# Second feed-forward on tiles of 128 rows, its norm computed during the attention

## Chip, cores and metric

One NeuronCore of a Trainium2 chip runs one program. The metric is the device time of one execution in microseconds (us); lower is better. Several runs of a kernel give a median.

## What is computed

x has 32 batches of 112 rows of 256 numbers, the context 32 batches of 375 rows of 256. Four layers follow one another, each added to x: an attention with one head over the context, a feed-forward of six linear maps, an attention with 16 heads over the context, and a second feed-forward. The last two are what the change touches:

```python
x = x + _L1_xattn_ref(ctx_1024, _layernorm(x), w_q, w_kv, w_out, b_out)      # 16 heads of 16
x = x + _L1_ffn_ref(_layernorm(x), norm1_w, w1, act_scale, act_bias, norm2_w, w2)

def bitlinear(x, norm_w, w):
    x_norm = rmsnorm(x, norm_w)                     # x / sqrt(mean(x*x) + 1e-8) * norm_w
    x_q = activation_quant(x_norm)                  # per row: round(x * 127 / max|x|), clipped, scaled back
    w_q = weight_quant(w)                           # -1, 0 or 1, times mean|w|
    return einsum('bsd,hd->bsh', x_q, w_q)
h = bitlinear(x, norm1_w, w1)                       # 256 -> 1024
h = act_scale * square(relu(h)) + act_bias
y = bitlinear(h, norm2_w, w2)                       # 1024 -> 256
```

## The kernel before

The program writes out the instructions of five engines by hand: TensorE (`pe`), ScalarE (`act`), VectorE (`dve`), GpSimd (`pool`) and SyncE (`sp`), which issues every DMA. Each engine executes its own list in order; a semaphore wait holds all that stands behind it on that engine. Four stages are separated by `stage_end` (L283), at which each engine waits for all others: setup, first attention, first feed-forward with the queries, second attention; the second feed-forward comes last.

x lies in SBUF for the whole program as `xs` (tile name x_stream), 112 partitions by 32 batches by 256. So every step works on one batch, 112 of 128 partitions.

**Second attention.** One step per batch b (`over_thirds`, three sets of buffers, loops of three batches). TensorE (`step3`, L1699) weaves the scores of batch b with `scores_for_max` of the batches b+1 and b+2, the weighing of the values, and the end of batch b-1: `fin_rows`, `fin_turn`, `fin_project`. VectorE takes the maxima of the score rows (`maxima`, L1188), splits them in three bf16 parts (`parts_m`), normalises the heads (`norm_o`), adds the output to x (`x4`, L1211, which raises `x_after_attn2`) and takes its statistics (`stats4`, `aggregate4`, `keep4`). GpSimd lays out the values (`lay_v`, L645) and computes from the statistics the factors of the later norm (`factors4`, L653, six linked operations on one column). `scores` of a batch needs `minus_max_in_place`: the row maxima, copied by ScalarE (`m_out`) and moved into `qs` by one small DMA (`rows_m`, L495).

SyncE runs `moves` (L512) for each batch:

```python
            def moves(b, par, n):
                more = not isinstance(b, int) or b < B - 3
                if more:
                    sp.wait_ge(shifted_scores_made, 12 * b + 6)
                    load_half(b + 3, par, 0)      # six DMAs
                if not isinstance(b, int) or b < B - 1:
                    rows_m(b + 1, (par + 1) % 3)
                if more:
                    sp.wait_ge(shifted_scores_made, 12 * b + 12)
                    load_half(b + 3, par, 1)      # six DMAs
```

**Second feed-forward.** After the barrier SyncE loads the two norm vectors. Per batch: GpSimd applies the norm to the row (`rms_x`, L713, three operations of 256 columns) and computes the root of the hidden norm (`hidden`, L726). VectorE finds the row maximum, rounds and clips (`max_x`, `factor_x`, `factors_x`, `round_x`, `clip_x`). TensorE turns the rows (`in_turn`), ScalarE copies them (`xq_out`), TensorE multiplies (`in_product`). ScalarE: `relu`, `square`, `squares` (sum of squares). VectorE: `activate` (L1277), `weigh_h` (L1306), `max_h` (L1310), `factors_h`, ScalarE `shift_up`, VectorE `clip_h`, TensorE `out_turn`, ScalarE `hq_out` (L919), TensorE `out_product` (L1757), VectorE `result` (L1337), SyncE `store_out`. In its step TensorE (L1765) runs `in_turn(b+1)`, `in_product(b+1)`, `out_product(b-2)`, `out_turn(b-1)`. VectorE's step (L1343) runs the twelve kinds above for the batches b+2, b, b-1 and b-2.

Of the kernel before, what the change touches and what calls it, by code (L numbers as in the profile page):

```python
# [11 lines left out]
P = 128  # L12
# [5 lines left out]
def xattn_ffn_kernel(  # L18
# [8 lines left out]
    TC = 3  # L27
# [17 lines left out]
    LN_EPS, RMS_EPS, Q_EPS = 1e-5, 1e-8, 1e-5  # L45
    assert TP * TC == T and KS + 3 <= P and NG % 2 == 0 and B % 2 == 0

    kd = nc.dram_tensor("k_parts_dram", [B, 3, DH, H, T], BF16, kind="Internal").ap()
    qd = nc.dram_tensor("q_parts_dram", [3, B, KC, DH, H8, L], BF16, kind="Internal").ap()

    with ExitStack() as ctx:
# [16 lines left out]
        w1T = sb("w1T", [P, KC, HID], BF16)  # L68
        w2T = sb("w2T", [P, HC, D], BF16)
# [6 lines left out]
        rs4, t4, rr4 = (sb(n, [L, B]) for n in ("rs4", "t4", "rr4"))  # L76
        eps4 = sb("eps4", [P, 2])
# [15 lines left out]
        wffT = eb("wffT", [P, NLIN, KC, D])  # L93
        b1parts = eb("b1parts", [P, NBLK, D], BF16)
# [51 lines left out]

        s3 = ExitStack()
# [8 lines left out]
        pvs = b3("pvs", [P, HQ, L])  # L156
        on = b3("on", [L, D])
        rden = b3("rden", [L, H])
        oT = pvs[:, 0:KC, :]
        nm = b3("nm", [L, H])  # L160
        nres = b3("nres", [L, H])
        npart = b3("npart", [L, 6 * H], BF16)
        mrow = b3("mrow", [6 * H, L], BF16)
        bs3 = b3("bs3", [L, 6])
        mv3 = b3("mv3", [L, 2])
# [3 lines left out]
        def b4(name, shape, dt=F32):  # L169
            return alloc(s4, name, shape, dt)  # L170
        n1_bc = b4("n1_bc", [P, D])
        n2_bc = b4("n2_bc", [P, HID])
        sc4 = b4("sc4", [L, B])
        nms4 = b4("nms4", [L, B])
        fw = b4("fw", [P, 2])
        y4 = [b4(f"y4{i}", [L, D]) for i in range(2)]
        xr4 = b4("xr4", [L, D])
        yw4 = b4("yw4", [L, D])
        am4 = [b4(f"am4{i}", [L, 13]) for i in range(2)]
        xq4 = b4("xq4", [L, D])  # L180
        xqT = b4("xqT", [P, KC, L], BF16)
        th = [b4(f"th{i}", [L, HID]) for i in range(2)]
        uh = [b4(f"uh{i}", [L, HID]) for i in range(2)]
        gh = [b4(f"gh{i}", [L, HID]) for i in range(2)]
        sq4 = b4("sq4", [L, HID])
        hq4 = b4("hq4", [L, HID])
        roundc = b4("roundc", [P, 1])
        hqT = b4("hqT", [P, HC, L], BF16)
        ot4 = [b4(f"ot4{i}", [L, D]) for i in range(2)]
        s4.close()  # L190


        at = [0]
# [1611 lines left out]
```

## Time and profile before

| | |
|---|---|
| median of 3 runs | 1369.27 us (1363.68 to 1371.06) |
| the profiled execution | 1369.87 us |
| its span | 1368.1 us |
| busy: TensorE, VectorE, ScalarE, GpSimd | 1172.6, 960.0, 596.2, 443.6 us |
| second attention | about 738 to 1130 us |
| second feed-forward | about 1134 to 1368 us |

The page of the profile gives the busy share of each engine in forty slices of the span, the granted TensorE clock (PEclk, 1.00 is 2.4 GHz, 0.50 is 1.2 GHz) and what the DMA engines moved. The timeline lists instructions by their start, with a bracket for the idle time before them and what ended it; SPq marks the instructions with which SyncE issues a DMA. Groups by form collect all instructions of one line and shape, with the mean duration. L numbers are lines of the kernel; L1405 is a helper that several products share.

### The profile page before, as it was taken

How to read it: one execution, taken by the hardware profiler on the slowest of the kernel's cores; microseconds unless marked ns; L12 is line 12 of the kernel's file. 1: busy time of each engine (PE TensorE's matmuls, PEld its weight loads, DVE VectorE, ACT ScalarE, POOL GpSimd, SP SyncE). 2: the span in 40 equal slices, each digit the busy share in tenths (PEclk: the TensorE clock that was granted, in tenths of full speed). 3: DMA queues.
4: the chain of work that ended last, by engine and by line, in shares of the span. 5: the costliest groups of instructions: out<-in, count | busy, mean ns of one | idle time of the engine just before them, and what ended most of it. 6: DMA issues, size and time to landing. Idle time of an engine off the chain costs nothing. (4 is left out here: it accounts for less than half of the span.)

```text
span 1368.1 us, 30729 instructions
## 1 busy us (share of the span) xinstructions
PE 1172.6 (86%) x9322; PEld 799.6 (58%) x9322; DVE 960.0 (70%) x2495; ACT 596.2 (44%) x1009; POOL 443.6 (32%) x792
## 2 busy tenths in 40 slices
PE   2799999999996989889666999999999993666766
PEld 2677777887775566565432555555555551444544
DVE  3556656666654666675556788888888864999996
ACT  1322232322231111111242556565565663888886
POOL 0334444444432221221113122222222224454451
PEclk7599999999998999999896999999999995777786
DMA  9323333223320000000069556566565610000000
GB/s 222 93 57 89 94 96 88 84 84 91 95 83 17 1 0 0 0 0 1 14 146 168 118 121 126 116 127 129 117 125 116 130 25 19 14 20 17 17 17 24
DMA packets 105310, 99.26 MB, mean 73 GB/s; under 512 B 43923, under 2 KB 98742, under 8 KB 105270
## 3 DMA queue, kind: packets, MB, share of 16 engines
q1 hardware_dynamic: 105270, 98.76, 31.3%
q8 instruction: 20, 0.33, 0.1%
q14 instruction: 20, 0.16, 0.0%
HBM read 70.76 MB, written 27.61 MB: 72 GB/s over the span
## 5 line engine op out<-in xcount | busy, mean ns | idle before, releaser
L1190 DVE TENSOR_REDUCE nm<-bank 112x1 f32<-112x375 f32 x512 | 269.9, 545 | 41.5 <-PE bank L1645 37.3
L864 ACT ACTIVATE pT<-bank 125x448 f32<-125x448 f32 x384 | 202.1, 543 | 96.6 <-PE bank L1661 93.8
L1645 PE MATMUL bank<-ks,qs 96*128 96x375 bf16 x512 | 171.5, 338 | 18.7 <-POOL qs L681 17.1
L1675 PE MATMUL bank<-pT,vaug 125*32 125x112 f32 x3072 | 152.7, 272 | 0.0
L1661 PE MATMUL bank<-qs,ks 128*128 128x112 bf16 x1536 | 141.8, 215 | 3.3 <-DMA qs<-mrow 3.0
L1661 PEld LDWEIGHTS bank<-qs,ks 128*128 128x128 bf16 x1536 | 97.6, 99 | 47.5 <-issue 31.2
L1675 PEld LDWEIGHTS bank<-pT,vaug 125*32 125x32 f32 x3072 | 60.7, 108 | 72.3 <-issue 59.7
L815 ACT ACTIVATE yT<-bank,bcol,gcol 128x448 f32<-128x448 f32 x48 | 32.2, 721 | 160.3 <-PE bank L1545 160.3
L1563 PE MATMUL bank<-wffT,hT 128*112 128x256 f32 x384 | 99.3, 392 | 0.0
L1405 PE MATMUL bank<-wv1T,ctxT 128*125 128x256 f32 x384 | 88.0, 379 | 0.0
L1405 PE MATMUL bank<-ctxT,wk1T 128*128 128x375 f32 x256 | 86.0, 478 | 0.0
L1089 DVE BATCH_NORM_STATS2 bs<-bank 112x6 f32<-112x256 f32 x96 | 36.6, 423 | 64.7 <-PE bank L1563 64.7
L1405 PEld LDWEIGHTS bank<-wv1T,ctxT 128*125 128x125 f32 x384 | 71.9, 187 | 17.3
L666 POOL TENSOR_TENSOR t<-mv,eps 112x1 f32 (+1 forms) x32 | 6.1, 191 | 230.1 <-DVE mv L1229 230.1
L1645 PEld LDWEIGHTS bank<-ks,qs 96*128 96x128 bf16 x512 | 50.2, 99 | 51.5 <-issue 39.6
L796 ACT ACTIVATE pr<-bank,ebias 112x375 f32<-112x375 f32 x32 | 18.4, 573 | 141.1 <-DVE ebias L1041 141.1
L1405 PE MATMUL bank<-yT,wffT 128*128 128x448 f32 x192 | 76.2, 540 | 0.1
L1545 PE MATMUL bank<-ident,yn 112*128 112x112 f32 x320 | 41.8, 278 | 37.9 <-DVE yn L1098 20.7
L1563 PEld LDWEIGHTS bank<-wffT,hT 128*112 128x112 f32 x384 | 64.0, 184 | 15.8 <-issue 1.8
L1405 PE MATMUL bank<-w1T,xqT 128*112 128x512 bf16 x128 | 48.9, 522 | 26.4 <-ACT xqT L917 26.4
L1545 PEld LDWEIGHTS bank<-ident,yn 112*128 112x128 f32 x320 | 34.1, 149 | 57.9 <-DVE yn L1098 35.9
L1405 PEld LDWEIGHTS bank<-ctxT,wk1T 128*128 128x128 f32 x256 | 48.4, 189 | 32.8
(210 smaller groups left out, 2451.3 us busy)
## 6 DMA issues: line engine op xcount, KB each, us to landing
k_parts_dram<-kp SPq DMA_DIRECT2D x192, 93.8 KB, 3.5
ks<-k_parts_dram SPq DMA_DIRECT2D x64, 281.2 KB, 4.2
cnat<-in_ctx_dram SPq DMA_DIRECT2D x32, 375.0 KB
ks<-k_parts_dram SPq DMA_DIRECT2D x64, 187.5 KB, 4.0
ks<-k_parts_dram SPq DMA_DIRECT2D x64, 93.8 KB, 3.3
q_parts_dram<-qp SPq DMA_DIRECT2D x48, 112.0 KB, 2.2
qs<-q_parts_dram SPq DMA_DIRECT2D x64, 84.0 KB, 4.0
x_stream<-in_x_dram SPq DMA_DIRECT2D x4, 896.0 KB, 13.0
```

Of the source, the lines that this page charges most:

```text
L666: link(pool.tensor_tensor(t4[:, at], v, eps4[0:L, 0:1], ALU.add))
L796: act.activation(pr[:, :], S1, ACT.Exp, bias=ebias[:, :], accum_out=psum_row[:, :]).then_inc(attn1_probs_made, 1)
L815: last = act.activation(yT[s][:, c, :], YT[s][:, c, :], ACT.Gelu, bias=bcol[:, k, c:c + 1], scale=gcol[:, k, c:c + 1])
L864: act.activation(pT[:, u % 4, :], B3[u % 3][0:TP], ACT.Exp).then_inc(probs_made, 1)
L1089: dve.bn_stats(bs2[s][:, t, :], LIN[s][:, t, :]).then_inc(lin_stats[s], 1)
L1190: dve.tensor_reduce(nm[:, h:h + 1], A3[h % 3][0:L], AX_X, ALU.max, negate=True).then_inc(head_max_taken, 1)
L1405: last = mm(o, lhs(k), rhs(k), start=(k == 0), stop=(k == KC - 1))
L1545: last = pe.transpose(YT[s][:, c, t * L:(t + 1) * L], yn[s][:, t, c * P:(c + 1) * P], ident[0:L, 0:L])
L1563: last = mm(LIN[s][:, t, :], hT[s][:, c, t * L:(t + 1) * L], wffT[:, 2 * k, c, :], start=False, stop=(c == KC - 1))
L1645: mm(A3[h % 3], qs[par][0:KS, h * L:h * L + P], ks[par][0:KS, h * T:(h + 1) * T], start=True, stop=True).then_inc(max_scores_made, 1)
L1661: last = mm(B3[c][:, j * L:(j + 1) * L], ks[par][:, h * T + c * TP:h * T + c * TP + P], qs[par][:, h * L:(h + 1) * L], start=True, stop=True)
L1675: last = mm(PV3[32 * j:32 * j + 32, g, :], vaug[par][:, c, h * VW:h * VW + 32], pT[:, u % 4, j * L:(j + 1) * L], start=(c == 0), stop=(c = ...
```

## The change

- **Tiles.** The 3584 rows are taken as 28 tiles of 128 rows (NT), across batch borders. As a batch lies on 112 partitions, rows go through memory: new `store_x` and `store_y` write each row block of x and of the normed x (y) to two DRAM tensors during the attention, and y is loaded back in four chunks of seven tiles (`load_y`), x in four chunks behind the attention. The buffers of the feed-forward lie now in `v_all`, whose first batches are used up by then, so most of them are free before the attention ends.
- **Norm.** `factors4` has eight linked operations instead of six, and `norm_y` (three operations of 256 columns on GpSimd, in place in `xs`) follows it in the attention's loop; it waits until x is stored. `rms_x` is gone.
- **Weights.** The two ternary weights are stored to DRAM after the setup and loaded again, with the second norm vector, in step 30 of the attention.
- **Barrier.** The `stage_end` behind the attention is gone on all engines; waits on single semaphores take its place. VectorE rounds tiles 0 and 1 ahead of `norm_o` of the last batch, TensorE runs `in_turn(0)` and `in_product(0)` ahead of its `fin_turn` and `fin_project`.
- **The work per tile.** The two clips are gone; the roundings write the result directly; `shift_up` on ScalarE becomes `round_h` on VectorE; `weigh_h` moves to GpSimd; `max_h` of tile i-1 stands at the head of VectorE's step i. Constants are folded into `k4`.
- **Order on TensorE:** `in_turn(i+1)`, `in_product(i+1)`, `out_turn(i-1)`, `out_product(i-1)`.

The core of the diff:

```diff
@@ SyncE, attention @@
+            def store_x(b):
+                sp.wait_ge(x_after_attn2, b + 1)
+                apart(sp, passed_sp)
+                if not isinstance(b, int) or b >= 1:
+                    sp.wait_ge(x_stored, 16 * b)
+                apart(sp, passed_sp)
+                sp.dma_start(xd[row(b)].rearrange("o l d -> l (o d)"),
+                             xs[:, row(b), :].rearrange("p o d -> p (o d)")).then_inc(x_stored, 16)
+
+            def store_y(b):
+                sp.wait_ge(y_made, b + 1)
+                apart(sp, passed_sp)
+                sp.dma_start(yd[row(b)].rearrange("o l d -> l (o d)"),
+                             xs[:, row(b), :].rearrange("p o d -> p (o d)")).then_inc(y_stored, 16)
+
+            def load_y(c, stored):
+                sp.wait_ge(y_stored, 16 * stored)
+                if c >= 1:
+                    sp.wait_ge(y_tiles_in, 16 * c)
+                sp.dma_start(yt4[:, c * CH:(c + 1) * CH, :], tiles_of(yd, c)).then_inc(y_tiles_in, 16)
...
-            def moves(b, par, n):
+            def moves(b, par):
                 more = not isinstance(b, int) or b < B - 3
+                if not isinstance(b, int) or b >= 2:
+                    store_y(b - 2)
+                if not isinstance(b, int) or b >= 1:
+                    store_x(b - 1)
                 if more:
                     sp.wait_ge(shifted_scores_made, 12 * b + 6)
                     load_half(b + 3, par, 0)
...
+                if isinstance(b, int) and b >= B - 3:
+                    load_y(b - (B - 3), b - 1)
+                if isinstance(b, int) and b == B - 2:
+                    sp.wait_ge(ffn2_weights_in, 16)
+                    everywhere_late(n2_bc, L1_ffn_norm2_w, HID)
+                    sp.dma_start(w1T4.rearrange("p k n -> p (k n)"), wd[0]).then_inc(ffn2_weights_in, 16)
+                    sp.dma_start(w2T4.rearrange("p c n -> p (c n)"), wd[1]).then_inc(ffn2_weights_in, 16)
...
+            store_y(B - 2)
+            store_x(B - 1)
+            sp.wait_ge(values_weighed, 12 * B)
+            sp.wait_ge(x_stored, 16 * B)
+            for c in range(NCH):
+                sp.dma_start(xt4[:, c * CH:(c + 1) * CH, :], tiles_of(xd, c)).then_inc(x_tiles_in, 16)
+            store_y(B - 1)
+            load_y(NCH - 1, B)
@@ GpSimd @@
+            def norm_y(b):
+                x_row = xs[:, row(b), :].rearrange("p o d -> p (o d)")
+                pool.wait_ge(x_stored, 16 * (b + 1))
...
+                pool.tensor_tensor(x_row, x_row, n1_bc[0:L, :], ALU.mult).then_inc(y_made, 1)
...
                     lay_v(3 * i + 3 + m, m, i)
                     factors4(3 * i + m)
+                    norm_y(3 * i + m)
...
+            def weigh_h(i, par):
+                pool.wait_ge(activation_made, i + 1)
+                if not isinstance(i, int) or i >= 2:
+                    pool.wait_ge(hidden_rounded, i - 1)
+                pool.tensor_tensor(gh[par], th[par], n2_bc, ALU.mult).then_inc(hidden_weighted, 1)
@@ ScalarE @@
+            def step4(i, par, n):
+                relu(i, par)
+                if not isinstance(i, int) or i < NT - 1:
+                    xq_out(i + 1)
+                square(i, par)
+                squares(i, par)
+                if not isinstance(i, int) or i >= 1:
+                    hq_out(i - 1)
@@ VectorE @@
+            def max_h(i, par):
+                dve.wait_ge(hidden_weighted, i + 1)
...
+            def step4(i, par, n):
+                past = not isinstance(i, int) or i >= 1
+                more = not isinstance(i, int) or i < NT - 2
+                if past:
+                    max_h(i - 1, 1 - par)
+                if more:
+                    max_x(i + 2, par)
+                if past:
+                    factor_h(i - 1, 1 - par)
+                if more:
+                    factor_x(i + 2, par)
+                if past:
+                    inverse_h(i - 1, 1 - par)
+                if more:
+                    inverse_x(i + 2, par)
+                if past:
+                    scale_h(i - 1, 1 - par)
+                    out_factor(i - 1, 1 - par)
+                    round_h(i - 1, 1 - par)
+                activate(i, par)
+                if more:
+                    round_x(i + 2, par)
+                if not isinstance(i, int) or i >= 2:
+                    result(i - 2, par, n - 1)
...
             over_thirds(dve, step3)
+            dve.wait_ge(ffn2_constants_made, 3)
+            dve.wait_ge(y_tiles_in, 16 * (NCH - 1))
+            for i in range(2):
+                max_x(i, i)
+                factor_x(i, i)
+                inverse_x(i, i)
+                round_x(i, i)
             norm_o(B - 1)
...
-            stage_end(dve, "dve", 4)
...
+            for i in range(2):
+                step4(i, i % 2, i // 2)
+            dve.wait_ge(x_tiles_in, 16 * NCH)
+            with dve.Fori(0, (late - 2) // 2) as i:
+                step4(2 * i + 2, 0, i + 1)
+                step4(2 * i + 3, 1, i + 1)
+            dve.wait_ge(y_tiles_in, 16 * NCH)
@@ TensorE @@
+            def step4(i, par, n):
+                if not isinstance(i, int) or i < NT - 1:
+                    in_turn(i + 1, 1 - par)
+                    in_product(i + 1, 1 - par)
+                if not isinstance(i, int) or i >= 1:
+                    out_turn(i - 1, 1 - par)
+                    out_product(i - 1)
```

## Rows read from the trace of the kernel before

**Rows 1.** Windows: us, busy PE, PEld, DVE, ACT, POOL; PEclk, DMA share, GB/s

```profile
900.00:1000.00 100.00, 99.82 (x1398) 58.40 (x1399) 84.94 (x213) 59.94 (x123) 28.27 (x69) 1.00 0.60 124
1160.00:1350.00 190.00, 129.99 (x650) 94.54 (x650) 182.71 (x467) 165.47 (x208) 90.47 (x142) 0.78 0.06 17
```

**Rows 2.** Timeline (start us, us, engine, line) of one attention batch

```profile
912.79 0.37 PE L1661 MATMUL bank<-qs,ks 128*128 128x112 bf16 x4
...
916.68 0.58 SPq L488 DMA_DIRECT2D ks<-k_parts_dram  x1
...
918.18 0.42 DVE L1215 TENSOR_TENSOR x_stream<-bank,x_stream 112x256 f32 x1 [0.94 <-PE bank L1405]
...
920.20 0.37 SPq L491 DMA_DIRECT2D qs<-q_parts_dram  x1
...
922.63 0.83 SPq L498 DMA_DIRECT2D qs<-mrow  x1
...
924.98 0.37 PE L1661 MATMUL bank<-qs,ks 128*128 128x112 bf16 x4
```

**Rows 3.** Timeline: row maxima behind a full queue, and the batch that follows

```profile
748.27 0.81 SPq L498 DMA_DIRECT2D qs<-mrow  x1
...
752.23 0.37 PE L1661 MATMUL bank<-qs,ks 128*128 128x112 bf16 x4 [1.59 <-DMA qs<-mrow]
...
765.95 0.37 PE L1661 MATMUL bank<-qs,ks 128*128 128x112 bf16 x4
```

**Rows 4.** Timeline: last of the six linked GpSimd operations of factors4

```profile
914.35 0.55 POOL L671 TENSOR_TENSOR rr<-t,minus_half 112x1 f32 x1 [0.25 <-POOL t L670]
```

**Rows 5.** Groups by form, GpSimd, whole execution: busy us, mean ns of one

```profile
L724 POOL TENSOR_TENSOR y<-y,n_bc 112x256 f32<-112x256 f32 x32 | 30.9, 965 | 2.5
...
L652 POOL TENSOR_TENSOR x_stream<-x_stream,bout_bc 112x256 f32 x27 | 19.6, 726 | 0.0
...
L589 POOL TENSOR_TENSOR kp<-kr,kp 128x750 bf16<-128x750 f32 x32 | 48.4, 1513 | 2.6
```

**Rows 6.** Groups by form, 1110 to 1370 us: VectorE and ScalarE

```profile
L1312 DVE TENSOR_REDUCE am<-gh 112x1 f32<-112x1024 f32 x32 | 38.5, 1204 | 0.0
...
L1275 DVE TENSOR_SCALAR hq<-uh 112x1024 f32<-112x1024 f32 x32 | 21.7, 678 | 0.0
...
L921 ACT ACTIVATE hqT<-bank 128x896 bf16<-128x896 f32 x32 | 29.0, 907 | 5.9 <-PE bank L1754 5.9
...
L1318 DVE TENSOR_SCALAR am<-am 112x1 f32<-112x1 f32 x32 | 6.5, 202 | 0.2
```

**Rows 7.** Timeline of feed-forward steps and of the last x

```profile
1133.86 0.42 DVE L1215 TENSOR_TENSOR x_stream<-bank,x_stream 112x256 f32<-112x256 f32 x1 [3.00 <-PE bank L1405]
...
1154.01 0.81 DVE L1280 TENSOR_SCALAR th<-uh,act_scale_col,act_bias_col 112x1024 f32<-112x1024 f32 x1 [3.32 <-ACT uh L902]
...
1256.48 1.07 PE L1405 MATMUL bank<-w1T,xqT 128*112 128x512 bf16 x4 [0.88 <-ACT xqT L917]
...
1259.29 0.99 PE L1754 MATMUL bank<-ident,hq 112*128 112x112 f32 x8 [0.86 <-DVE hq L1275]
...
1262.43 0.80 DVE L1280 TENSOR_SCALAR th<-uh,act_scale_col,act_bias_col 112x1024 f32<-112x1024 f32 x1
```

**Rows 8.** Timeline of the end: last activation, last product, last result

```profile
1351.43 0.80 DVE L1280 TENSOR_SCALAR th<-uh,act_scale_col,act_bias_col 112x1024 f32<-112x1024 f32 x1
...
1363.09 1.95 PE L1762 MATMUL bank<-w2T,hqT 128*112 128x256 bf16 x8 [1.01 <-ACT hqT L921]
...
1365.14 0.48 DVE L1340 SCALAR_TENSOR_TENSOR ot<-bank,am,x_stream 112x256 f32<-112x256 f32 x1 [4.86 <-issue]
```

**Rows 9.** Page: GB/s in forty slices; DMA view: stores of results

```profile
GB/s 222 93 57 89 94 96 88 84 84 91 95 83 17 1 0 0 0 0 1 14 146 168 118 121 126 116 127 129 117 125 116 130 25 19 14 20 17 17 17 24
...
out_dram<-ot SPq DMA_DIRECT2D x32, 112.0 KB, 1.9
```

More of the change, by code:

```diff
@@ new lines, in _ @@
+            with dve.Fori(0, (NT - 2 - late) // 2) as i:
+                step4(2 * i + late, 0, i + late // 2)
+                step4(2 * i + late + 1, 1, i + late // 2)
+            for i in range(NT - 2, NT):
+                step4(i, i % 2, i // 2)
+            max_h(NT - 1, 1)
+            factor_h(NT - 1, 1)
+            inverse_h(NT - 1, 1)
+            scale_h(NT - 1, 1)
+            out_factor(NT - 1, 1)
+            round_h(NT - 1, 1)
+            result(NT - 2, 0, NT // 2 - 1)
+            result(NT - 1, 1, NT // 2 - 1)
@@ L1730, in _, with in_turn, in_product @@
                 scores_for_max(1, 1, 0, h)
+            def in_turn(i, par):
+                pe.wait_ge(x_rounded, i + 1)
+                for k in range(KC):
+                    last = pe.transpose(XT4[:, k, :], xq4[par][:, k * P:(k + 1) * P], ident[:, :])
+                last.then_inc(x_int_turned, 1)
+            def in_product(i, par):
+                pe.wait_ge(x_intT_ready, i + 1)
+                if not isinstance(i, int) or i >= 2:
+                    pe.wait_ge(relu_made, i - 1)
+                for half in range(2):
+                    last = over_rows(H4[par][:, half * 512:(half + 1) * 512], lambda k: xqT[:, k, :],
+                                     lambda k: w1T4[:, k, half * 512:(half + 1) * 512])
+                last.then_inc(hidden_made, 1)
@@ new lines, in out_turn, with out_product @@
+            def out_turn(i, par):
+                pe.wait_ge(hidden_rounded, i + 1)
+                for c in range(HC):
+                    last = pe.transpose(HT4[:, c // 4, (c % 4) * P:(c % 4 + 1) * P], hq4[par][:, c * P:(c + 1) * P], ident[:, :])
+                last.then_inc(hidden_int_turned, 1)
+            def out_product(i):
+                pe.wait_ge(hidden_intT_ready, i + 1)
+                if not isinstance(i, int) or i >= 1:
+                    pe.wait_ge(result_made, i)
+                for c in range(HC):
+                    last = mm(Y4, hqT[:, c, :], w2T4[:, c, :], start=(c == 0), stop=(c == HC - 1))
+                last.then_inc(ffn2_out_made, 1)
@@ L1778, in _ @@
[L1778 removed]
+            pe.wait_ge(x_after_attn2, B)
+            over_tiles(pe, step4, 2, 2)
+            out_turn(NT - 1, 1)
+            out_product(NT - 1)
 _INS = ['x', 'ctx_1024', 'L0_xattn_Wq', 'L0_xattn_bq', 'L0_xattn_Wk', 'L0_xattn_bk', 'L0_xattn_Wv', 'L0_xattn_bv',
```

464 lines of the change are left out of this document (195 added, 269 removed).

## The prediction, made before the changed kernel ran

> **What bounds the kernel now.** I read the page's forty slices first, then the windows view by stage, then one attention step and one feed-forward step in the timeline, and last the views by form for the durations. The times of the profile are from one execution: its span is 1368.1 us, its own time 1369.87 us, so 1.8 us lie outside the span, and it is 0.6 us above the median of 1369.27 us.
>
> The second attention (738 to 1130 us) is bound by TensorE: 99.82 of 100 us are busy, with the clock granted in full [rows 1]. One batch takes 12.2 us from its first score product to that of the next batch (912.79 to 924.98) [rows 2]. The second feed-forward (1133 to 1368) is bound by VectorE; the engine to watch besides is TensorE, whose granted clock there is well under 1 [rows 1], so its products run now at 2.4, now at 1.2 GHz. The 31 steps from the first activation (1154.01) to the last (1351.43) take 197.4 us, 6.37 each [rows 7, 8].
>
> **Attention: what SyncE now has to wait for.** In `moves(b)` the change puts `store_y(b-2)` and `store_x(b-1)` ahead of the six loads of `load_half(b+3)` and ahead of `rows_m(b+1)`, the small transfer of the row maxima without which the scores of batch b+1 can't start. SP is one queue of instructions, so both stand behind `store_x`, which waits for `x_after_attn2` of batch b-1. Read from the step's beginning (912.79 = 0): before, the first of six loads is issued at 3.9, the last at 7.4 (done at 7.8), SP then idles 2 us and issues the maxima at 9.84, and TensorE starts the next batch at 12.19, which is 2.35 us after the issue [rows 2]. There is no wait recorded at that start, so the transfer comes just in time, with next to no slack.
>
> After: x of batch b-1 is finished only at 5.8 (918.18 + 0.42) [rows 2]. Semaphore, register work and the issue of one store I take as 1.0 us (a small DMA is issued in 0.37, and the next one follows 0.2 later), so the loads begin at 6.8 instead of 3.9. The burst lasts 4.0 us, the maxima go out at 10.8 to 10.9 instead of 9.84, and the next batch starts at 10.9 + 2.35 = 13.25. That is 1.1 us a batch, on TensorE, on the path. It holds for the batches 1 to 28, which still load: 28 x 1.1 = +31 us. Bounds: 0.85 (a quicker issue) gives +24; the maxima now leave right behind the loads, not 2 us later, and where the queue was full (maxima issued at 748.27, scores at 752.23) they took 3.96 us [rows 3]; of that I allow at most another 0.6 a batch, +48.
>
> `store_y(b-2)` is not the later one: the six linked operations of `factors4` end 2.1 us into the step (914.35 + 0.55) [rows 4]. Two links (0.8 us) and three operations of 256 columns (0.6 to 0.73 each, 2.4 with their links) are added, and since the step is longer while the statistics stay where they were, y is there at about 4.4, stored before x is ready at 5.8. GpSimd is then late for `lay_v` by 4 us, which is not used for two batches. The 64 stores of 112 KB land in 1.9 us each [rows 9] beside a DMA share of 0.60 [rows 1]: free. So are the weights' way through memory and the copy of the norm's vector.
>
> **The hand-over.** Before, x of the last batch is added at 1133.86 and the first activation is at 1154.01 [rows 7, 8]: barrier, two vectors loaded, the norm. After, in the time base of before: the weights and y's second quarter (2.4 MB at about 222 GB/s [rows 9], 11 us) are issued in step 30 and the third quarter behind them, so y is there at about 1134.5. Two tiles are rounded first (2 us), and only then comes `norm_o(31)`; `in_product(0)` stands before `fin_project` on TensorE. I get x of the last batch at 1142, its statistics at 1143.6, the first activation at 1144.5: -9.5 us.
>
> **The loop of the feed-forward.** 28 tiles instead of 32 and less work per tile on VectorE (the two clips and the weighting are gone): by its own work it would need some 5 us. But two loops of waits now are longer than that.
>
> (a) `weigh_h` goes to GpSimd, and VectorE's next step begins with `max_h`, which needs it. Activate 0.80, to GpSimd 0.2, weigh W, `max_h` 1.20, `max_x` behind it 0.25, small linked steps 0.75 (0.2 each, fillers between), `round_h` 0.68 (as the clip) [rows 6, 7], then the next activation. W for 1024 columns with two tensors: 256 columns take 0.73, 750 take 1.51 [rows 5]; their slope gives 1.95, four times the short one 2.9; I take the middle, 2.4. The loop is 6.3 us (5.8 to 6.8).
>
> (b) TensorE's order is now in_turn, in_product, out_turn, out_product of the same tile, so ScalarE's copy stands between the last two, where before `out_product` took a tile whose copy was long made. Per tile: in_turn 0.4, copy 0.35, in_product 1.07, out_turn 0.99 x 128/112 = 1.13, copy 0.91 x 8/7 = 1.04, out_product 1.05, hand-offs 0.2: 5.3 us at the full clock. At the lower one the products take 1.95 and the turn about 2.0 [rows 6, 7, 8]: 8.2 us.
>
> So a tile takes 6.3 us when the clock is full and 8.2 when it is not. The granted clock of 0.78 before [rows 1] means 56% of the time at the full level; TensorE's work per us stays about the same, so I keep it: 1/(0.56/6.3 + 0.44/8.2) = 7.0 us. 27 steps make 189. One more wait: VectorE waits ahead of step 2 for all of x (3.67 MB, 17 us at 222 GB/s), and these loads start only when x of the last batch is stored (1144.5); x is there at 1162, the step could start at 1155: +7. Together 196 against 197.4: -1.4. The gain of fewer tiles is spent.
>
> **Tail.** From the last activation to the last result: 13.7 before [rows 8]; after 0.8 + 0.2 + 2.4 + 1.2 + 0.75 + 0.7, a turn and a product at mixed clock 3.1, a copy 1.04: 10.2 to 10.4, -3.3.
>
> **Sum.** +31 - 9.5 - 1.4 - 3.3 = +16.8; span 1384.9, time 1386.7; less 0.6 for the median: 1386 us.
>
> **A rule against the change.** GpSimd's multiplication of y with two tensors takes 0.965 us on average for the 256 columns for which the same form in the attention takes 0.726 [rows 5]; the longer ones lie under VectorE's operations. The Trainium skill (GPSIMD Engine Reference, section 3.1 and the specifications) says that elementwise work of two tensors is about twice as slow there as on VectorE, 4497 ns for 2048 columns, and that GpSimd shares SBUF interfaces with VectorE and contends with certain of its modes. By the page's figure (an estimate, half of it) W would be 2.25 and loop (a) 6.15, near my value; by its warning W is longer, the first slow rival below. The rows show both.
>
> **Rivals.**
> 1. *The store of x delays nothing* (faster). SP gets through x's store soon enough, or the maxima have slack that I don't see. For it: SP idles 2 us before the maxima, so only a delay over about 1.9 us counts, and mine is 2.9. Against: both ends are from the timeline. Without it the time is 1386 - 31 = 1355. It decides below a delay of 1.9. Chance 0.13.
> 2. *TensorE's clock stays full in the feed-forward.* Loop (a) alone, 6.3: 27 x 0.7 = -19, 1367. Against: TensorE idles as much as before. 0.13.
> 3. *GpSimd is slow* (slower). At the rate of the 0.965 row W is 3.9, loop (a) 7.8; against 8.2 at the lower clock that gives about 7.9: 27 x 0.9 = +24, 1410. 0.14.
> 4. *The gap costs TensorE its clock in the attention* (slower). After one gap of 1.6 us (to 752.23) the batch took 13.7 us (to 765.95) instead of 12.2 [rows 3]. If every second gap of about 1.1 us does it, 14 x 1.5 = +21, 1407; if each does, 1428. Against: the gaps are shorter. 0.15.
> My forecast, 1375 to 1400, has 0.45.
>
> **Chances.** A measurement of this kernel can tell about 0.5% from no change, 1362.4 to 1376.1 us. Faster: rival 1, 0.13. Same: rival 2 and the lower edge of the forecast, 0.15. Slower 0.72. The range 1358 to 1420 leaves out most of rival 1 and the far end of rival 4.
>
> **What would show it.** Right: TensorE waits about 1 us per batch for the maxima's transfer, SP issues them at 10.8 us of a step of 13.2, right behind six loads that begin after x's store; attention's TensorE share falls to about 92%; in the feed-forward VectorE waits about 2 us per tile for GpSimd's product, TensorE about 1 us for ScalarE's copy ahead of `out_product`, tiles of 6.3 and of 8.2 us; a stop of about 7 us before tile 2. Wrong: batches of still 12.2 us, or W far from 2.4, or tiles under 6.5 on average.

## The result, and the profile after

The changed kernel takes 1375.65 us (median of 20 runs, 1370.01 to 1384.99); the kernel before, in 20 runs beside it, 1368.05 us (1363.68 to 1375.23). The ratio is 1.0057, with a 95% interval of 1.0039 to 1.0076. The forecast was slower, 1386 us: the direction is right and the time lies in the range, but the slowdown is less than half of the one forecast (7.6 us against 16.7). The profiled execution has a span of 1371.9 us (before: 1368.1).

The page of the changed kernel: busy times, TensorE's granted clock in forty slices, and three groups (busy us, mean ns | idle time before it and who ended it).

```profile
PE 1140.0 (83%) x9221; PEld 765.4 (56%) x9234; DVE 883.2 (64%) x2318; ACT 546.9 (40%) x953; POOL 501.3 (37%) x875
...
PEclk7699999999998999999886999999999999599887
...
L1737 PE MATMUL bank<-qs,ks 128*128 128x112 bf16 x1536 | 142.3, 216 | 41.3 <-DMA qs<-mrow 41.3
...
L807 POOL TENSOR_TENSOR v_all<-v_all 128x1024 f32<-128x1024 f32 x28 | 66.2, 2365 | 80.7 <-DVE v_all L1358 80.7
...
L1363 DVE TENSOR_REDUCE v_all<-v_all 128x1 f32<-128x1024 f32 x28 | 34.1, 1220 | 58.0 <-POOL v_all L807 58.0
```

The first group is the score products of the second attention: TensorE now stands idle ahead of them for 41.3 us in all, and the row maxima's transfer ends it. The second is GpSimd's new weighting of the hidden row, 2.365 us each; the third is the maximum behind it, for which VectorE waits 58.0 us.

The windows view, to be read beside [rows 1] (us, busy PE, PEld, DVE, ACT, POOL; PEclk, DMA share, GB/s):

```profile
900.00:1000.00 100.00, 87.76 (x1234) 50.47 (x1227) 75.33 (x189) 51.92 (x107) 40.79 (x96) 1.00 0.58 126
1200.00:1330.00 130.00, 76.69 (x446) 49.44 (x456) 89.94 (x250) 97.46 (x126) 63.69 (x61) 0.89 0.08 26
```

The second window in the kernel before:

```profile
1200.00:1330.00 130.00, 87.78 (x443) 64.22 (x442) 124.56 (x323) 112.59 (x143) 64.84 (x100) 0.79 0.06 18
```

TensorE's share in the attention fell from 99.82 to 87.76 of 100 us, with the clock still granted in full. In the steady part of the feed-forward (1200 to 1330 us) the granted clock rose from 0.79 to 0.89, and VectorE, which had bound that stage with 124.56 of 130 us, is busy for 89.94, which is 69%.

One attention batch of the changed kernel, from its first score product to that of the next (timeline; the answer to [rows 2]):

```profile
959.04 0.37 PE L1737 MATMUL bank<-qs,ks 128*128 128x112 bf16 x4 [1.49 <-DMA qs<-mrow]
...
964.44 0.42 DVE L1289 TENSOR_TENSOR x_stream<-bank,x_stream 112x256 f32 x1 [0.94 <-PE bank L1481]
...
965.28 0.34 SPq L532 DMA_DIRECT2D x_rows_dram<-x_stream  x1
...
965.93 0.63 SPq L510 DMA_DIRECT2D ks<-k_parts_dram  x1
...
969.49 0.36 SPq L513 DMA_DIRECT2D qs<-q_parts_dram  x1
969.97 0.84 SPq L520 DMA_DIRECT2D qs<-mrow  x1
...
972.93 0.37 PE L1737 MATMUL bank<-qs,ks 128*128 128x112 bf16 x4 [1.67 <-DMA qs<-mrow]
```

Counted from 959.04, x is finished at 5.8, its store goes out at 6.2, the six loads run from 6.9 to 10.8, the maxima are issued at 10.9 and the next batch starts at 13.9. From 822 us on the batches last 13.3 to 14.0 us, 13.65 on average, instead of 12.2.

The hand-over to the feed-forward (the answer to [rows 7]):

```profile
1181.74 0.42 DVE L1289 TENSOR_TENSOR x_stream<-bank,x_stream 112x256 f32<-112x256 f32 x1 [4.35 <-PE bank L1481]
...
1184.31 0.81 DVE L1358 TENSOR_SCALAR v_all<-v_all,ffn_constants,act_bias_col 128x1024 f32<-128x1024 f32 x1 [0.33 <-ACT v_all L988]
...
1189.23 0.72 POOL L766 TENSOR_TENSOR x_stream<-x_stream,n_bc 112x256 f32<-112x256 f32 x1 [0.18 <-POOL x_stream L763]
1189.91 2.34 POOL L807 TENSOR_TENSOR v_all<-v_all 128x1024 f32<-128x1024 f32 x1
...
1192.28 1.22 DVE L1363 TENSOR_REDUCE v_all<-v_all 128x1 f32<-128x1024 f32 x1 [6.89 <-POOL v_all L807]
...
1195.10 0.81 DVE L1358 TENSOR_SCALAR v_all<-v_all,ffn_constants,act_bias_col 128x1024 f32<-128x1024 f32 x1
```

The first activation comes 2.6 us after the last x. The second is 10.8 us behind it, not 6.2: GpSimd does the factors and the norm of the last batch first (the last operation of it at 1189.23), and only then the first weighting.

A tile of the steady part, then a spell of TensorE at its lower level, and the end (timeline):

```profile
1264.31 0.81 DVE L1358 TENSOR_SCALAR v_all<-v_all,ffn_constants,act_bias_col 128x1024 f32<-128x1024 f32 x1
...
1265.27 2.35 POOL L807 TENSOR_TENSOR v_all<-v_all 128x1024 f32<-128x1024 f32 x1 [3.00 <-DVE v_all L1358]
...
1267.66 1.22 DVE L1363 TENSOR_REDUCE v_all<-v_all 128x1 f32<-128x1024 f32 x1 [1.89 <-POOL v_all L807]
...
1270.49 0.81 DVE L1358 TENSOR_SCALAR v_all<-v_all,ffn_constants,act_bias_col 128x1024 f32<-128x1024 f32 x1
...
1285.23 1.89 PE L1833 MATMUL bank<-v_all 128*128 128x256 bf16 x8 [1.12 <-ACT v_all L1000]
...
1288.09 1.89 PE L1481 MATMUL bank<-v_all 128*128 128x512 bf16 x4 [0.55 <-ACT v_all L969]
1289.77 1.91 PE L1825 MATMUL bank<-ident,v_all 128*128 128x128 f32 x8
1292.88 1.04 PE L1833 MATMUL bank<-v_all 128*128 128x256 bf16 x8 [1.19 <-ACT v_all L1000]
...
1297.90 1.05 PE L1833 MATMUL bank<-v_all 128*128 128x256 bf16 x8 [1.30 <-ACT v_all L1000]
...
1358.14 0.81 DVE L1358 TENSOR_SCALAR v_all<-v_all,ffn_constants,act_bias_col 128x1024 f32<-128x1024 f32 x1
...
1369.17 0.48 DVE L1394 SCALAR_TENSOR_TENSOR v_all<-bank,v_all,x_tiles 128x256 f32<-128x256 f32 x1 [4.67 <-PE bank L1833]
```

From one activation to the next are 6.18 us: the loop through GpSimd. In the spell from 1285.23 on, all of TensorE's operations take nearly twice as long, and one round of its own loop, `out_product` to `out_product`, takes 7.65 us. The round behind it takes 5.02. The activations around them (1282.87, 1289.08, 1295.54, 1301.87) are 6.2, 6.5 and 6.3 us apart: the slow round has cost 0.4 us.

The spans of the two profiled executions, side by side:

| part | before | after | difference | forecast |
|---|---|---|---|---|
| start to step 31 of the attention | 1119.97 | 1159.98 | +40.0 | +31 |
| step 31 to the first activation | 34.04 | 24.33 | -9.7 | -9.5 |
| first to last activation | 197.4 | 173.8 | -23.6 | -1.4 |
| last activation to the end | 16.7 | 13.8 | -2.9 | -3.3 |
| sum | 1368.1 | 1371.9 | +3.8 | +16.8 |

### The profile page after: what moved, and what is told of

Read it like the earlier page. It is cut to its first block, busy times and chain, and to the rows that moved or that the text cites. A ratio compares the mean times of both kernels' runs of the same rounds, so it can differ in the third digit from the quotient of the medians.

```text
span 1371.9 us, 30853 instructions
## 1 busy us (share of the span) xinstructions
PE 1140.0 (83%) x9221; PEld 765.4 (56%) x9234; DVE 883.2 (64%) x2318; ACT 546.9 (40%) x953; POOL 501.3 (37%) x875
## 4 chain that ended last, share of the span: by engine, by line
PE 51%; SPq 12%; DVE 11%; issue 10%; DMA 7%; POOL 5%; ACT 2%; DVEq 1%; POOLq 0%; ACTq 0%
PE bank L1481 23%; PE bank L1639 6%; DMA qs<-mrow 5%; SPq L510 4%; PE bank L1737 4%; SPq L513 3%; PE bank L1575 3%; PE bank L1721 3%; POOL v_all L807 3%; PE bank L1751 3%; DVE hT L1183 2%; PE bank L1564 2%; DVE yn L1172 1%; POOL rs L706 1%; PE bank L1833 1%
## 5 line engine op out<-in xcount | busy, mean ns | idle before, releaser
L1737 PE MATMUL bank<-qs,ks 128*128 128x112 bf16 x1536 | 142.3, 216 | 41.3 <-DMA qs<-mrow 41.3
L807 POOL TENSOR_TENSOR v_all<-v_all 128x1024 f32<-128x1024 f32 x28 | 66.2, 2365 | 80.7 <-DVE v_all L1358 80.7
L704 POOL TENSOR_SCALAR ve<-mv 112x2 f32<-112x2 f32 x48 | 10.6, 220 | 169.5 <-DVE mv L1142 169.5
L1363 DVE TENSOR_REDUCE v_all<-v_all 128x1 f32<-128x1024 f32 x28 | 34.1, 1220 | 58.0 <-POOL v_all L807 58.0
## 6 DMA issues: line engine op xcount, KB each, us to landing
ks<-k_parts_dram SPq DMA_DIRECT2D x64, 187.5 KB, 3.9
```

The lines of the kernel that those rows point to most:

```text
L807: pool.tensor_tensor(gh[par], th[par], n2_bc, ALU.mult).then_inc(hidden_weighted, 1)
L1737: last = mm(B3[c][:, j * L:(j + 1) * L], ks[par][:, h * T + c * TP:h * T + c * TP + P], qs[par][:, h * L:(h + 1) * L], start=True, stop=True)
```

## The experiments

The kernel before, run beside each group of experiments, took 1367.9, 1370.14 and 1368.98 us. Single times below (where no interval stands) are one execution each.

**Both stores behind the maxima.** In SP's program, `moves(b)`:

```diff
-                store_y(b - 2)
-                store_x(b - 1)
                 load_half(b + 3)
                 rows_m(b + 1)
+                store_y(b - 2)
+                store_x(b - 1)
```

> The changed kernel with store_y(b-2) and store_x(b-1) moved behind rows_m(b+1) in moves; the same transfers, another place in SyncE's order. Theory O (order: the loads and the row maxima stand behind the wait for x): a batch of the attention goes back from 13.65 us to 12.2 to 12.3 us, TensorE's wait for the maxima falls from 41 us to under 6, and the time from 1375.65 to about 1336 us (1330 to 1345). Rival T (traffic: 64 more stores keep the queue so full that loads and maxima land late wherever the stores stand): batches stay at 13.3 us or more and the time at 1366 us or more.

Measured: 1336.42 us, ratio to before 0.9773 (0.974 to 0.9805); span 1331.0. Its window, its row of the maxima's wait, and its activations:

```profile
900.00:1000.00 100.00, 99.64 (x1394) 58.00 (x1394) 84.03 (x211) 59.42 (x123) 46.50 (x107) 1.00 0.67 143
...
L1737 PE MATMUL bank<-qs,ks 128*128 128x112 bf16 x1536 | 141.3, 215 | 3.8 <-DMA qs<-mrow 2.8
...
L1358 DVE TENSOR_SCALAR v_all<-v_all,ffn_constants,act_bias_col x28: 806/808/816, 1142.6 to 1317.2; 128x1024 f32<-128x1024 f32 x28
```

TensorE is as full as in the kernel before, the idle time for the maxima is 3.8 us instead of 41.3, the batches last 12.2 to 12.3 us, and the first activation is at 1142.6 instead of 1184.3. The stores still move the same bytes (143 GB/s against 124 before, [rows 1]), so neither their traffic nor GpSimd's norm costs the attention anything. All of it was the place in SP's queue. The feed-forward is as long as in the changed kernel (174.6 against 173.8).

**Only the store of x behind the maxima**, `store_y` left in front:

```diff
                 store_y(b - 2)
-                store_x(b - 1)
                 load_half(b + 3)
                 rows_m(b + 1)
+                store_x(b - 1)
```

> Only store_x(b-1) is moved behind rows_m(b+1); store_y(b-2) stays in front of the loads. Theory O says that each store costs what its own wait costs: y is ready 5.4 us into an unstretched batch, the first load then goes out near 6.2 instead of 3.9, and batch and wait settle at 12.7 us (+0.5 a batch, +14 us against the kernel with both moved; time about 1350 us). Rival Y (y is always ready in time, as the prediction had it): the same as with both moved, 12.2 to 12.3 us and about 1336 us.

Measured: 1348.54 us. Batches last 12.4 to 13.3 us, 12.7 on average:

```profile
900.00:1000.00 100.00, 95.81 (x1351) 55.55 (x1351) 81.97 (x207) 57.65 (x120) 43.34 (x102) 1.00 0.65 138
```

So about two thirds of the attention's loss come from x's store and one third from y's, once x's no longer stands behind it (one execution). The prediction had y's store as free; it is free only in the shadow of x's.

**The weighting on VectorE**, right behind the activation:

```diff
 GpSimd:  -                weigh_h(i, par)
 VectorE:                  activate(i, par)
          +                weigh_h(i, par)
```

> The changed kernel with weigh_h back on VectorE, behind activate and ahead of round_x; GpSimd keeps only root_h. Theory G (the tile of 6.27 us is the loop activate, GpSimd's product, max_h, round_h): VectorE no longer waits 1.85 us a tile, its own work remains, 5.5 to 5.9 us a tile on average, 27 steps shorter by 10 to 20 us, time about 1360 us. Rival B (TensorE's loop with ScalarE's copies is the longer one, as the prediction's 7.0 us assumed, and 6.27 is its mixture over the clock's levels): tiles stay at 6.2 us or more, time within 4 us of 1375.65.

Measured: 1354.72 us, 21 us under the changed kernel. The activations, from the first to the last, and the head of VectorE's step 2 (timeline):

```profile
L1357 DVE TENSOR_SCALAR v_all<-v_all,ffn_constants,act_bias_col x28: 805/808/814, 1181.9 to 1339.2; 128x1024 f32<-128x1024 f32 x28
...
1195.19 1.22 DVE L1368 TENSOR_REDUCE v_all<-v_all 128x1 f32<-128x1024 f32 x1 [2.08 <-DMA x_tiles<-x_rows_dram]
```

The stage is 157.4 us long against 173.8. From the second activation (1190.78) on a tile takes 5.7 us on average; the same 26 steps take 6.27 each in the changed kernel. The loop through GpSimd was what set the tile; VectorE, which does the product in 1.23 us, is now the bound (126.08 of 130 us busy from 1200 to 1330 us). The second line shows the wait for all of x ahead of step 2, which the prediction had named: 2.1 us here.

**TensorE's order of before**: `out_product(i-2)` ahead of `out_turn(i-1)`, so that no copy of ScalarE stands between a turn and its product.

```diff
                     in_product(i + 1, 1 - par)
+                if not isinstance(i, int) or i >= 2:
+                    out_product(i - 2)
                     out_turn(i - 1, 1 - par)
-                    out_product(i - 1)
```

> The changed kernel with TensorE's order of before: out_product(i-2) ahead of out_turn(i-1), so that no product stands right behind the copy it needs. Theory G: nothing changes, tiles 6.2 to 6.3 us, time within 4 us of 1375.65; TensorE's wait of 1.1 us ahead of out_product is gone but it waits elsewhere. Rival B: loop (b) of the prediction loses about 1.1 us, tiles fall to 6.0 us or less and the time by 7 us or more.

Measured: 1392.56 us, 17 us slower than the changed kernel, which neither theory had. In the spans 13.7 us of it lie in the stage from first to last activation (187.5 against 173.8) and 5.1 ahead of it. The window, the activations, and one tile:

```profile
1200.00:1330.00 130.00, 87.13 (x410) 54.17 (x411) 84.26 (x229) 86.35 (x113) 59.13 (x57) 0.74 0.09 31
...
L1358 DVE TENSOR_SCALAR v_all<-v_all,ffn_constants,act_bias_col x28: 805/807/815, 1189.4 to 1377.0; 128x1024 f32<-128x1024 f32 x28
...
1254.99 1.81 PE L1833 MATMUL bank<-v_all 128*128 128x256 bf16 x8
...
1257.11 0.48 DVE L1394 SCALAR_TENSOR_TENSOR v_all<-bank,v_all,x_tiles 128x256 f32<-128x256 f32 x1 [1.79 <-PE bank L1833]
...
1260.15 1.89 PE L1481 MATMUL bank<-v_all 128*128 128x512 bf16 x4 [2.25 <-ACT v_all L969]
...
1261.01 0.81 DVE L1358 TENSOR_SCALAR v_all<-v_all,ffn_constants,act_bias_col 128x1024 f32<-128x1024 f32 x1
```

The three gaps of TensorE (0.6 to 1.2 us each) have become one of 2.25 us in every tile, and the granted clock is 0.74 instead of 0.89. Both products behind the gap run at the lower level (1.89 and 1.81), and VectorE waits 1.8 us for the second one ahead of `result` and so ahead of `max_h`. From the second activation (1200.18) to the last a tile takes 6.80 us.

**The same order with the gap filled**: eight extra transposes in the gap ahead of `in_product`; they are dummy work and their results are overwritten.

```diff
+                for _ in range(8):
+                    pe.transpose(H4[par][:, 0:P], ident[:, :], ident[:, :])
                 pe.wait_ge(x_intT_ready, i + 1)
```

> TensorE's order of before in the changed kernel, as in e4_pe_order (tiles of 6.95 us, granted clock 0.74, one gap of 2.25 us per tile ahead of in_product), with eight transposes of the identity as filler in that gap; they go to columns that in_product overwrites. Theory C (what made e4_pe_order 17 us slower is the clock that TensorE lost through its one long gap): the granted clock rises to 0.85 or more and tiles fall to 6.6 us or less, although TensorE has 1.1 us more to do. Rival R (the order itself, result behind two products): the clock stays at 0.74 or rises without help, tiles stay at 6.9 us or more.

Measured: 1375.21 us, 17 us faster than without the extra work; 15.4 of these lie between first and last activation. The window, the second activation, the last one (in the group's line):

```profile
1200.00:1330.00 130.00, 86.90 (x622) 64.83 (x631) 90.60 (x251) 96.14 (x126) 64.87 (x63) 0.99 0.08 28
...
1198.58 0.81 DVE L1358 TENSOR_SCALAR v_all<-v_all,ffn_constants,act_bias_col 128x1024 f32<-128x1024 f32 x1
...
L1358 DVE TENSOR_SCALAR v_all<-v_all,ffn_constants,act_bias_col x28: 806/808/814, 1187.4 to 1359.6; 128x1024 f32<-128x1024 f32 x28
```

The clock is granted nearly in full, the gap is down to 1.2 to 1.4 us, and the 26 steps from 1198.58 to 1359.6 take 6.19 us each. With the clock back, the order of before costs nothing against the changed kernel's (6.27), and 6.19 us is the loop through GpSimd by itself.

**The changed kernel with the turn done twice.** In `out_turn` the eight transposes are issued twice (dummy work, 1.09 us of TensorE a tile, inside its own loop).

```diff
-                for c in range(HC):
+                for c in [*range(HC), *range(HC)]:
```

> The changed kernel with the eight transposes of out_turn issued twice (1.09 us more of TensorE's work per tile at the full clock). Measured so far: a tile takes 6.27 us bound by the loop over GpSimd (it falls to 5.8 with the product on VectorE), so TensorE's own loop, 5.3 us at the full clock by the prediction's sum, should have about 0.9 us to spare. Theory G: 5.3 + 1.1 = 6.4, so tiles of 6.4 to 6.8 us, +4 to +15 us, time near 1385. Rival B (no slack, the loops' mixture over the clock's levels counts in full): +1.1 a tile or more, 7.4 us, +30 us, time near 1406.

Measured: 1382.01 us. In the steady part the activations are still 6.18 to 6.22 us apart, with a granted clock of 0.95 in the window of 1200 to 1330 us; from the second activation (1202.40) to the last (1367.3) it is 6.34 a tile, and what is above 6.2 lies in the first two of these steps (8.65 and 7.62), where the clock is at its lower level (it is there from 1180 to 1214 us). More than a microsecond of work more on TensorE costs the steady tile nothing. The span is 8.3 us longer (1380.2 against 1371.9), and 7.3 of these lie ahead of the first activation (1191.6 against 1184.3), where the two kernels are the same. The trace shows what differs there: five batches of the attention of this run, those from 794.05, 946.46, 961.59, 1086.56 and 1128.69, begin with a spell at the lower level (granted clock 0.59 from 947 to 951 us, for one) and last 14.8 to 15.3 us instead of 13.65. In the changed kernel there is one such batch behind the first step, from 806.78, with 15.7 us.

**The changed kernel with a filled gap.** Six extra transposes (dummy work) ahead of `in_product`, in TensorE's order of the changed kernel.

```diff
+                for _ in range(6):
+                    pe.transpose(H4[par][:, 0:P], ident[:, :], ident[:, :])
                 pe.wait_ge(x_intT_ready, i + 1)
```

> The changed kernel with six extra 128 by 128 transposes in each tile of the second feed-forward (dummy work: their results are overwritten), put ahead of in_product, where TensorE waits for xq_out anyway (0.8 us a tile); everything else as in the changed kernel, GpSimd's weigh_h and both stores included. It adds some 1.6 us of TensorE work a tile and closes one of its three gaps. Theory G (the loop through GpSimd sets the tile; TensorE's spells at the lower clock lie in its slack): granted clock from 1200 us on rises from 0.89 to 0.97 or more, tile stays 6.2 to 6.3 us, time within 4 us of the changed kernel, 1372 to 1380. Rival M (the prediction's mixing: the time of a tile follows the share of time at the lower clock): the tiles at the lower level shorten, the stage gets 5 to 8 us shorter, time 1366 to 1370. Rival B (TensorE's own work sets the tile): 0.8 us or more a tile longer, time 1395 or more.

Measured: 1373.74 us, ratio to before 1.0029 (1.001 to 1.0048). The clock rose less than expected, to 0.92 in the window of 1200 to 1330 us; the stage from first to last activation is 173.4 us against 173.8. It is the time of the theory in which the spells lie in slack, but because the clock moved so little this run by itself is a weak witness; the filled order of before, at 0.99, is the strong one.

**The two remedies together**: both stores behind the maxima, and the weighting on VectorE (the first and the third diff).

> Both repairs together: the stores behind the row maxima and weigh_h on VectorE. If the two effects are independent, the attention keeps its 12.25 us batches and the tiles their 5.8 us: 1336.4 - 21 = about 1315 us (1311 to 1320). If they share a cover (say the clock, or transfers that now meet the feed-forward), 1325 or more.

Measured: 1319.66 us, ratio to before 0.9634 (0.9598 to 0.9671). It beats both kernels, by 50 us (the kernel before beside it: 1370.14) and 56 us. That is 5 us above the 1315 expected: the 21 us that the expectation took off were those between two single executions, of which 16.5 lay between first and last activation, and 1336.4 - 16.5 is 1320. A tile takes mostly 5.5 us, but some take 5.7 to 6.5, where TensorE is at its lower level (granted clock 0.90 from 1200 to 1330 us); from the third activation (1164.47) to the last (1306.27) the mean is 5.67.

**The same, with six extra transposes a tile** (dummy work, as above).

> The version with both stores behind rows_m and with weigh_h on VectorE (1319.7 us), and the same six extra transposes in each tile (dummy work). Its tiles last 5.8 us with VectorE nearly without idle time and a granted clock of 0.90. If VectorE sets the tile: clock 0.98 or more, tile 5.7 to 5.85, time 1316 to 1323. If the lower clock of TensorE still costs something there (0.91 at 1280 to 1300, 0.64 at 1300 to 1320 us): 1308 to 1314. If TensorE's work sets it: 1335 or more.

Measured: 1317.54 us, ratio to before 0.9615 (0.9583 to 0.9647), which can't be told from the version without them. The clock is 0.96 from 1200 to 1330 us. From the third activation (1166.68) to the last a tile takes 5.52, so that the spells at the lower level cost 25 x 0.15, about 4 us of that stage. Here VectorE leaves less slack than GpSimd's round trip does in the changed kernel; the gain is too small for the times to show it.

**The product split**, 512 columns on GpSimd and 512 on VectorE at the same time, with both stores behind the maxima:

```diff
 GpSimd:  +                pool.tensor_tensor(gh[par][:, 0:512], th[par][:, 0:512], n2_bc[:, 0:512], ALU.mult)
 VectorE: +                dve.tensor_tensor(gh[par][:, 512:HID], th[par][:, 512:HID], n2_bc[:, 512:HID], ALU.mult)
```

> As e9_late_and_weigh, but the product is split: GpSimd takes columns 0 to 511, VectorE 512 to 1023, in the same time. GpSimd's half ends 0.2 + 1.2 us after activate, when VectorE is through with its own half, round_x and result (1.4 us). Theory: VectorE's work falls to 5.0 us a tile and TensorE's loop of 5.3 us becomes the bound: tiles of 5.3 to 5.5 us, about 10 us less than e9_late_and_weigh, near 1305. Rival P (VectorE and GpSimd hinder each other while both read two tensors from SBUF): both halves stretch, tiles of 5.8 us or more, time at or above that of e9_late_and_weigh.

Measured: 1343.02 us, ratio 0.9813 (0.9776 to 0.985): 23 us slower than with the whole product on VectorE, and no better than with the whole product on GpSimd (1336.42). Two groups by form from 1220 to 1310 us (busy us, mean ns | idle), and one tile:

```profile
L808 POOL TENSOR_TENSOR v_all<-v_all 128x512 f32<-128x512 f32 x14 | 24.2, 1731 | 51.6 <-DVE v_all L1360 47.7 <-ACT v_all L997 3.9
...
L1354 DVE TENSOR_SCALAR v_all<-v_all 128x256 f32 x14 | 19.0, 1356 | 0.0
...
1265.29 0.69 DVE L1367 TENSOR_TENSOR v_all<-v_all 128x512 f32<-128x512 f32 x1
1265.41 1.69 POOL L808 TENSOR_TENSOR v_all<-v_all 128x512 f32<-128x512 f32 x1 [3.88 <-ACT v_all L997]
...
1265.89 1.36 DVE L1354 TENSOR_SCALAR v_all<-v_all 128x256 f32 x1
...
1267.57 1.20 DVE L1372 TENSOR_REDUCE v_all<-v_all 128x1 f32<-128x1024 f32 x1
```

Half of GpSimd's product takes 1.73 us, not half of 2.365 (1.18, an estimate): it starts at 1265.41 while VectorE's half runs until 1265.98. And `round_x`, which takes 0.35 us in the changed kernel (at 1265.03 there), takes 1.36: it ends at 1267.25, just behind GpSimd's product (1267.10). The two engines hold each other up in turn. The Trainium skill (SBUF — State Buffer, section "Who interferes with whom") says that a VectorE operation with two inputs in SBUF, or a one-input copy or tensor-scalar operation in a two-port mode, contends with GpSimd for one pair of ports, and that the second to come is blocked until the first ends. The trace agrees in both directions: GpSimd's product is late by about VectorE's half, and `round_x` ends only when GpSimd's product has ended. `result`, which has an input in PSUM, kept its 0.47 us. In the changed kernel the two hardly meet: `round_x` ends 0.1 us after GpSimd's product has begun (1265.38 and 1265.27), `result` has its input in PSUM, and for the rest VectorE waits idle while GpSimd weighs.

## Why the prediction was right or wrong

**What bounds each stage, before.** Right as read: [rows 1] shows TensorE in the attention and VectorE in the feed-forward, and the windows of the changed kernel show VectorE no longer the bound there.

**Attention, +31 forecast, +40.0 measured.** The mechanism was right at every row: x at 5.8, loads from 6.8 (6.9), maxima issued at 10.9 (10.9). Moving the stores gave back 39 us (1375.65 to 1336.42), so all of it comes from where the stores stand. The term that was mis-sized is the last one, the 2.35 us from the issue of the maxima to the next batch, which the sum took over from [rows 2]: it is 2.96 (969.97 to 972.93) where the maxima leave 0.1 us behind the last load. Where they leave 1.3 us after it, as in the run with late stores, it is 2.39 (955.83 to 958.22). Over the 28 batches that load it is 2.8 on average (2.4 to 3.3), against 2.4 before. So a batch costs 1.4 us more, not 1.1; 28 x 1.4 = 39. About 2 us of the 40 are something else, the spell of the clock at 807 us (rival 4 below). The prediction had named this very risk and put up to 0.6 a batch in the range, and it was 0.6 in the batch shown and 0.4 on average; it should have been in the central value, since the prediction itself had the maxima leave right behind the loads. That the loads just ahead of it are what delays the transfer is inferred from the order of the rows; no run changed the distance alone.

`store_y` as free: right in the changed kernel, wrong as a statement by itself (0.5 us a batch once x's store is out of the way).

**The hand-over, -9.5 forecast, -9.7 measured.** Right in its sum. VectorE waited 8.5 us there for the y tiles and then rounded two of them.

**The feed-forward, -1.4 forecast, -23.6 measured.** This step failed. Its pieces were good: W 2.365 against 2.4, loop (a) 6.19 against 6.3, loop (b) 5.02 at the full level and 7.65 for the round at the lower one against 5.3 and 8.2, waits of 1.9 us for GpSimd and 1.1 to 1.3 for ScalarE as told. What failed is how they were put together. The sum gave every tile the longer of the two loops at its clock level and averaged: 7.0 us. But the loops run beside each other, and a slow round of TensorE is followed by a fast one that catches up, 7.65 and then 5.02, while VectorE goes on at its 6.2. What counts is the mean of loop (b) against loop (a), not the mean of the larger. The 0.56 is a share of time, so the mean is taken as the prediction took it: with its own clock and the measured rounds, loop (b) takes 1/(0.56/5.02 + 0.44/7.65) = 5.9 us, and by the prediction's own pieces 1/(0.56/5.3 + 0.44/8.2) = 6.3. Loop (a), 6.2 measured and 6.3 forecast, would still have been the bound, or as good as that. These are estimates: no run had this order at a clock of 0.78.

The second part of the fault is the clock, kept at 0.78. It was 0.89 (before: 0.79 in the same window). The filled order tells what the remaining spells cost: 6.19 a tile at 0.99 against 6.27 from the second activation to the last (1195.10 to 1358.14) at 0.89, so 2 us in all. Nearly the 7.0 us did occur, but in a kernel that wasn't the changed one and by another path: the order of before, with its clock of 0.74, took 6.80. I had counted TensorE's new order as a cost (loop (b) has a copy in it) and not seen what it buys: it cuts one long gap into three short ones.

In numbers: 26 steps of 6.27 instead of 7.0 are -19; the first step took 10.8 instead of 7.0 + 7, -3. Together they are the whole difference to the forecast of this stage.

**The stop of 7 us for all of x.** As a wait for x it didn't show in the changed kernel. The loads were issued from 1184.28 on; step 2 began at 1198.40, when GpSimd's second product ended. The term was also too large: with the weighting on VectorE the wait appears, but it is 2.08 us, and it ends at 1195.19, 13.4 us after the first of these loads was issued (1181.81), not 17. The sum had taken 222 GB/s for them, and in the changed kernel 357 GB/s flowed from 1188 to 1192 us. What stopped the first tiles for 4.6 us is GpSimd, where the norm of the last batch stands ahead of the first weighting. The prediction had named GpSimd's queue for the attention and not for this place.

**The tail, -3.3 forecast, -2.9 measured.** Right.

**How the errors stood.** +9 in the attention and -22 in the feed-forward against the forecast make -13; the span rose by 3.8 instead of 16.8. A part of the attention's number is chance between executions: the first activation of kernels that are the same up to there was at 1184.3, 1186.3, 1187.4, 1189.4 and 1191.6. Two sources can be read: the attention starts earlier or later (its first maxima are issued at 735.84 in the changed kernel and at 741.12 in the filled order of before), and the number of batches with a spell at the lower clock differs, one in the changed kernel and five in the run with the turn done twice. That the time lay in the range although the feed-forward was 22 us off is in part luck: the attention's error had the other sign.

**The rivals.** 1 (the store of x delays nothing) is wrong: the delay is 1.4 us a batch. 2 (the clock stays full in the feed-forward, loop (a) alone) is the one that described that stage best, 27 x 6.3 = 170 us against 173.8, with the clock at 0.89 rather than full; its total of 1367 misses the attention's other 9 us. It had 0.13 because I argued that TensorE idles as much as before, which says nothing of how the idle time is cut. 3 (GpSimd slow, W 3.9) is wrong for this kernel, W 2.365. The Trainium skill (GPSIMD Engine Reference, section 3.1) gives 4497 ns for 2048 columns, an estimate of 2.25 us for 1024, which the trace bears out to about 5%. The warning of contention from the same page of the Trainium skill (the specifications) shows where the two engines work at the same time, as in the split product. 4 (the gap costs the clock in the attention) had a true mechanism and a much too large price. The batch of 13.7 us in [rows 3], on which it rested, was such a spell in the kernel before: right behind the gap that ends at 752.23 the granted clock is 0.57, and it is 0.98 from 756 us on (windows view).

```profile
752.20:756.00 3.80, 3.77 (x32) 2.79 (x32) 2.63 (x6) 2.13 (x4) 0.00 (x0) 0.57 0.63 112
```

The changed kernel has the same spell there (0.59 from 752 to 756 us) and one more, behind the gap of 1.52 us that ends at 806.78:

```profile
807.00:810.00 3.00, 3.00 (x24) 2.27 (x20) 2.28 (x5) 1.68 (x4) 1.93 (x5) 0.55 1.03 210
```

That batch took 15.7 us, 2 us more than the others. All 28 batches have a gap of this kind, 1.4 us on average, and the rival counted on 14 or 28 spells; from 900 to 1000 us the clock is 1.00 throughout.

**What would show it.** Of the signs listed, "tiles under 6.5 on average" was named as the one that would prove the forecast wrong, and it did.

## What to carry to other kernels

Before an instruction that waits is put into a queue, look at what stands behind it there: two stores that nobody waits for cost 39 us ahead of a small transfer for which TensorE waits, and nothing behind it. Where two loops of waits share a stage and buffers lie between them, compare their mean lengths, and let a slow round be made up by the fast one behind it; an average over the larger of the two overstates the time. When an operation is moved to an idle engine, price the round trip in the loop and not the busy time: 2.4 us on GpSimd against 1.2 on VectorE made the tile longer than it is with the product on VectorE (6.27 us against 5.7), though VectorE had become idle for nearly a third of the time.

## What the runs showed of the hardware

TensorE's granted clock depended on how its idle time was cut. The changed kernel and the one with TensorE's order of before give it the same work per tile. With gaps of 0.6 to 1.2 us in a tile the clock was 0.89, with one of 2.25 us it was 0.74; that TensorE is busy for more of the window there (87.13 of 130 us against 76.69) comes from products that take 1.89 us instead of 1.04. More work raised the clock too: 0.99 with that gap filled down to 1.2 to 1.4 us, where 17 us came back for adding work, and in the changed order 0.95 with the turn done twice and 0.92 with six extra transposes. In the attention a gap of 1.4 us on average in each batch of 13.65 us mostly left it at 1.00; single gaps were followed by a few microseconds at the lower level, one behind the first step in the changed kernel and five in the run with the turn done twice, each of which made its batch 1.2 to 2 us longer. What decides is open.

GpSimd and VectorE stretched each other's operations when they ran at the same time on SBUF: 0.35 to 1.36 us for a tensor-scalar operation of 256 columns, and 1.73 us for a GpSimd product whose half share of 2.365 is 1.18.
